# Router logits inside the layer norms, half of the router's one-hot factors as signs on ScalarE, and more buffers for the routed tiles

## The chip, the core and the metric

The kernel runs on one core of one Trainium2 chip. The metric is the device time of one execution in microseconds (us). Three runs of the kernel before gave a median of 1519.82 us (1518.86 to 1523.01). The engines are TensorE (PE in the profile, with PEld for its weight loads), VectorE (DVE), ScalarE (ACT), GpSimd (POOL) and SyncE (SP, which here only issues DMAs and waits). Each engine runs its own program in order, and they meet at semaphores.

## The reference, cut to what matters

Two transformer-like layers over 2048 tokens of width 256. Each is attention over a context, attention or a recurrence over the tokens, and a mixture of experts, and each sub-layer reads a layer norm of x and adds to x. The change touches the layer norms in front of the two mixtures and the mixtures themselves:

```python
# first mixture: x = x + _L0_ffn_ref(_layernorm(x), ...), T=2048, H=256, F=1024, E=8, TOP_K=2
logits = x @ Wg
probs = jax.nn.softmax(logits, axis=-1)
vals, idx = jax.lax.top_k(probs, TOP_K)
weights = vals / (jnp.sum(vals, axis=-1, keepdims=True) + EPS)
hpre = jnp.einsum('th,ehf->tef', x, W1) + b1
act = jax.nn.silu(hpre)
y = jnp.einsum('tef,efh->teh', act, W2) + b2
out = jnp.einsum('te,teh->th', cw, y)          # cw: weights at the chosen experts, else 0
shared = jax.nn.silu(x @ Ws1 + bs1) @ Ws2 + bs2
out = out + SHARED_SCALE * shared

# second mixture: x = x + _L1_ffn_ref(_layernorm(x), ...), E=16, I=192, TOPK=4
logits = jnp.einsum('nh,eh->ne', x, gate_w)
scores = jax.nn.sigmoid(logits)
sb = scores + gate_bias                        # two best groups of four, then four best experts
g = jnp.einsum('nh,eih->nei', x, w1)
u = jnp.einsum('nh,eih->nei', x, w3)
hact = jax.nn.silu(g) * u * combine[:, :, None]
y = jnp.einsum('nei,ehi->nh', hact, w2)
shared = jnp.einsum('ni,hi->nh', jax.nn.silu(x @ ws1.T) * (x @ ws3.T), ws2)
return y + shared
```

## The kernel before

The tokens lie in 16 tiles of 128 (`NT`), kept in SBUF as `k.x` through the whole kernel. A value that has to be exact beyond fp16 is split in two fp16 parts, high and low: ScalarE writes the high part with an ACTIVATE Copy, VectorE the low part as the difference.

The kernel is a chain of blocks, and all engines meet at the end of a block. The blocks that matter here, each once for each mixture:

- **`boundary`** is the layer norm. It goes in 8 steps of two tiles. In a step VectorE takes statistics (L302, L307), the reciprocal (L312) and the normalised rows `xn` (L317); ScalarE writes the high part of the rows (`high`, L258), VectorE the low part (`low`, L321); TensorE transposes both (L221), and ScalarE copies them from PSUM to `n` (`turned`, L266). The rows are also stored to `n_rows` in DRAM, from which the experts gather them later. Two `Boundary` arguments matter: `project`, a function that TensorE calls from its step 3 on, once all tiles of a group of four are in `n`, and `fetch`, which issues the first part of the expert weights.
- **`route`** turns the logits into a placement. TensorE computes the logits (L1025, 16 tiles of 6 small matmuls). Meanwhile ScalarE and VectorE split the first weight slots (`mix.early` of them: `cast_high` L950, `cast_low` L956). Then ScalarE makes the scores (the second mixture's sigmoid, L2134), VectorE chooses the experts (`choose`, from L1693 or L2139) and computes for each choice of each token a slot number, whose upper part (`hi`) says which tile and whose lower part (`lo`) says which row. To invert that map, VectorE writes two one-hot factors for each of the NT x K pairs (32 and 64): `hot_lo` (L1120, 128 wide, times the token's number) and `hot_hi` (L1121, 39 or 79 wide), and TensorE multiplies them into one accumulator (L1035). From it VectorE computes, in a tail (from L1125), the lists `token` and `dest` that the gathers and the scatters use.
- **`first_tiles`** and **`second_tiles`** run the experts. The second has 16 tiles of the shared expert, straight from `n`, and then 79 routed tiles. For these GpSimd gathers 128 rows of `n_rows` for each tile (L1540), TensorE turns them (L1409) and multiplies (L1421), ScalarE takes the SiLU (L1468), VectorE the product with the other half (L1500), the fp16 split of the hidden rows follows (for shared tiles the high part on ScalarE, L1473, for routed ones on VectorE, L1505; the low part L1510, L1511), TensorE turns and multiplies again (L1429, L1436 to L1440), VectorE writes `y` (L1521), and GpSimd scatters it to `y_rows` (L1544). GpSimd has `R` = 32 row buffers; it issues 28 gathers ahead of the first scatter and then mixes the other 51 with the scatters. `y` has 4 buffers, and VectorE waits at L1521 for the scatter that frees one (`t_stored`). The remaining 12 weight slots of the second mixture (17 in all, 1280 wide) are split during the first 12 shared tiles, one in each. At the block's end GpSimd waits for every `t_stored` semaphore.
- **`combine`** then reads `y_rows` back (SP's issues at L1588) and adds them to x with the weights.

In `second_tiles` the order of GpSimd's work comes from these lines:

```python
while gathered < min(R - 4 + (mix.tiles - R + 4) * (s + 1) // (mix.tiles - 12), mix.tiles):
    gather(gathered)
    gathered += 1
scatter(s)
```

## Time and profile before

| | us |
|---|---|
| median of three runs | 1519.82 (1518.86 to 1523.01) |
| profiled execution | 1519.53 |
| its span | 1517.7 |

The blocks around the two mixtures, in the profiled execution, from the span's start:

| block | from | to | us |
|---|---|---|---|
| boundary before the first mixture | 517.0 | 543.2 | 26.2 |
| route of the first mixture | 543.2 | 578.3 | 35.1 |
| tiles of the first mixture | 578.3 | 886.0 | 307.7 |
| boundary before the second mixture | 1138.8 | 1164.9 | 26.1 |
| route of the second mixture | 1164.9 | 1235.6 | 70.7 |
| tiles of the second mixture | 1235.6 | 1467.1 | 231.5 |
| block end and combine | 1467.1 | 1517.7 | 50.6 |

A row of a timeline has the start, the busy time, the engine, the line and operation, what it writes and reads, and in brackets the idle time ahead of it and what ended it. A row with xN stands for N instructions in a run, and its time is that of the whole run. Durations of neighbours overlap a little, so what one more instruction costs is the distance between starts, not the duration. PEclk is the granted clock of TensorE as a share of 2.4 GHz.

### The profile page before, as it was taken

Reading aid. Unit: us, or ns where it says so; the run is one execution under the profiler, and the core shown is the slowest. Engines: PE = TensorE matmul, PEld = TensorE weight load, DVE = VectorE, ACT = ScalarE, POOL = GpSimd, SP = SyncE. Lnnn points to the kernel's source line nnn. Section 1 sums busy time; section 2 is a strip of 40 time slices with the busy share of each in tenths; the row PEclk is TensorE's granted clock in tenths of the full one; section 3 lists DMA queues with packets and bytes.
Section 4 is the critical chain, followed back from the end, with each engine's and each line's share of the span. In section 5 each row is a group of like instructions: output and inputs, shape, how many; then the busy total and the mean of one; then the engine's idle time right before and its main releaser. Section 6 shows DMA issues by size and latency. Waiting matters only on the chain. (4 is left out here: it accounts for less than half of the span.)

```text
span 1517.7 us, 41010 instructions
## 1 busy us (share of the span) xinstructions
PE 1192.2 (79%) x13450; PEld 869.1 (57%) x13450; DVE 1023.9 (67%) x2922; ACT 823.7 (54%) x2124; POOL 450.0 (30%) x480
## 2 busy tenths in 40 slices
PE   5899999998699528999999965966892165999950
PEld 2688888886345417988888842522572033766630
DVE  5699999997656777975544537333657976666636
ACT  6688888885588535854444413411646025666520
POOL 0555555552300000013333210200020037677740
PEclk9999999999899758999999965977995569999975
DMA  3433333332000274001111148298005312233328
GB/s 95 99 78 81 77 81 81 79 79 72 1 1 0 80 294 194 2 16 51 51 51 49 42 149 261 66 350 269 25 1 213 139 35 63 79 105 102 103 71 274
DMA packets 111807, 150.27 MB, mean 99 GB/s; under 512 B 13625, under 2 KB 96962, under 8 KB 111682
## 3 DMA queue, kind: packets, MB, share of 16 engines
q1 hardware_dynamic: 95730, 112.80, 23.8%
q0 software_dynamic: 11328, 30.95, 6.7%
q10 hardware_dynamic: 4624, 4.85, 1.0%
q8 instruction: 78, 1.28, 0.4%
q14 instruction: 47, 0.39, 0.1%
HBM read 126.80 MB, written 21.76 MB: 98 GB/s over the span
## 5 line engine op out<-in xcount | busy, mean ns | idle before, releaser
L1266 ACT ACTIVATE mixture_and_attentions_h<-ps,mixture_and_attentions_b 128x128 f32<-128x128 f32 x440 | 125.6, 373 | 126.2 <-PE ps L1218 124.9
L1218 PE MATMUL ps<-xture_and_attentions_m_w 128*128 128x128 f16 x1872 | 155.7, 219 | 1.8 <-DVE xture_and_attentions_m_w L1296 1.8
L1218 PEld LDWEIGHTS ps<-xture_and_attentions_m_w 128*128 x1872 | 129.1, 98 | 36.2 <-issue 2.6
L1540 POOL DMA_INDIRECT tage_second_mixture_rows<-n_rows,e_second_mixture_r_token x79 | 90.2, 1141 | 140.5 <-SPq L1371 116.7
L641 POOL TENSOR_TENSOR ads_and_recurrence_ctx_s<-ads_and_recurrence_ctx_c,ads_and_recurrence_ctx_s 128x512 f16<-128x512 f32 x64 | 74.2, 1160 | 177.6 <-ACT ads_and_recurrence_ctx_s L570 177.6
L1304 DVE TENSOR_SCALAR ixture_and_attentions_hs<-mixture_and_attentions_h 128x512 f16<-128x512 f32 x110 | 47.2, 429 | 112.7 <-PE ps L1237 97.6
L590 ACT ACTIVATE ads_and_recurrence_probs<-ps,s_and_recurrence_neg_max 128x257 f32<-128x257 f32 x256 | 117.7, 480 | 1.1 <-DVE s_and_recurrence_neg_max L672 1.1
L1236 PE MATMUL ps<-xture_and_attentions_m_w,ixture_and_attentions_hs 128*128 x312 | 117.5, 379 | 0.2 <-DVE xture_and_attentions_m_w L1315 0.2
L1335 POOL DMA_INDIRECT ture_and_attentions_rows<-n_rows,e_and_attentions_r_token x39 | 38.8, 994 | 261.2 <-SPq L1173 162.7
L1421 PE MATMUL ps<-stage_second_mixture_m_w,stage_second_mixture_x_s 128*128 x474 | 92.3, 332 | 2.1 <-issue 1.9
L1544 POOL DMA_INDIRECT y_rows<-stage_second_mixture_y,ge_second_mixture_r_dest x79 | 77.6, 982 | 39.4 <-issue 21.6
L681 DVE TENSOR_SCALAR _heads_and_recurrence_pn<-ads_and_recurrence_probs,heads_and_recurrence_inv 128x256 f32<-128x256 f32 x256 | 79.9, 371 | 8.3
L1237 PE MATMUL ps<-xture_and_attentions_m_w,ixture_and_attentions_hs 128*128 x312 | 85.0, 273 | 0.0
L672 DVE TENSOR_REDUCE s_and_recurrence_neg_max<-ps 128x2 f32<-128x514 f32 x128 | 81.9, 679 | 2.1 <-PE ps L512 2.1
L487 PE MATMUL ps<-ads_and_recurrence_ctx_s,currence_wh_L_xattn_wk_t 128*128 128x256 f16 x512 | 78.3, 276 | 5.1 <-issue 5.1
L1306 DVE SCALAR_TENSOR_TENSOR ixture_and_attentions_hs<-mixture_and_attentions_h,ixture_and_attentions_hs 128x512 f16<-128x512 f32 x110 | 76.2, 693 | 3.8
L520 PE MATMUL ps<-consts_sb,_heads_and_recurrence_pn 128*128 128x128 f32 x512 | 77.0, 273 | 2.2 <-DVE heads_and_recurrence_p_t L688 2.2
L496 PE MATMUL ps<-currence_wh_L_xattn_wv_t,ads_and_recurrence_ctx_s 128*128 128x256 f16 x512 | 77.7, 275 | 0.0
L1339 POOL DMA_INDIRECT y_rows<-xture_and_attentions_m_w,re_and_attentions_r_dest x39 | 38.5, 988 | 131.5 <-DVE xture_and_attentions_m_w L1315 131.2
L635 POOL TENSOR_SCALAR ds_and_recurrence_mask_b<-ds_and_recurrence_mask_i 128x257 bf16<-128x257 int32 x64 | 70.2, 1097 | 5.4
L665 DVE TENSOR_SCALAR ads_and_recurrence_ctx_c<-ads_and_recurrence_ctx_t 128x256 f32<-128x256 f32 x128 | 62.6, 528 | 7.0 <-DMA ads_and_recurrence_ctx_t<-in_ctx_t 7.0
L582 ACT ACTIVATE e_heads_and_recurrence_v<-ps 128x512 f32<-128x512 f32 x64 | 38.2, 597 | 52.5 <-PE ps L531 50.8
(395 smaller groups left out, 3325.4 us busy)
## 6 DMA issues: line engine op xcount, KB each, us to landing
ads_and_recurrence_ctx_t<-in_ctx_t SPq DMA_DIRECT2D x64, 257.0 KB, 2.7
e_and_attentions_b_ctx_t<-in_ctx_t SPq DMA_DIRECT2D x14, 1028.0 KB, 9.2
ure_and_attentions_b_ctx<-in_ctx SPq DMA_DIRECT2D x28, 512.0 KB, 7.8
xture_and_attentions_m_w<-in_m_w SPq DMA_DIRECT2D x2, 5632.0 KB, 37.3
ds_and_recurrence_mask_i<-in_mask SPq DMA_DIRECT2D x256, 32.1 KB, 1.7
stage_second_mixture_c_y<-y_rows SPq DMA_DIRECT2D x16, 512.0 KB, 4.9
stage_second_mixture_m_w<-in_m_w SPq DMA_DIRECT2D x2, 3840.0 KB, 20.5
xture_and_attentions_m_w<-in_m_w SPq DMA_DIRECT2D x1, 5120.0 KB, 16.6
```

The costliest lines, as they stand in the source:

```text
L487: last = pe.matmul(ps[:, KB, m * KR:(m + 1) * KR], w[:, c, m * P:(m + 1) * P], x[:, c, :], start=(n_ == 0), stop=(n_ == len(products) - 1))
L496: last = pe.matmul(ps[:, VB, r * D:(r + 1) * D], x[:, c, r * P:(r + 1) * P], w[:, c, :], start=(n_ == 0), stop=(n_ == len(products) - 1))
L590: act.activation(probs[p][:, j, :], ps[:, SB + j, 0:SK], ACT.Exp, bias=neg_max[:, p, j:j + 1], accum_out=sums[:, p, j:j + 1]).then_inc(k.a ...
L672: dve.tensor_reduce(neg_max[:, p, 2 * h:2 * h + 2], ps[:, SB + 2 * h:SB + 2 * h + 2, 0:SK], AX.X, ALU.max, negate=True).then_inc(k.a_max.s ...
L681: last = dve.tensor_scalar(pn[p][:, j, :], probs[p][:, j, 0:KR], inv[:, p, j:j + 1], None, ALU.mult)
L1218: last = pe.matmul(ps[:, UB + 2 * (u % 2) + f // PER, (f % PER) * P:(f % PER + 1) * P], slots.of(e, c, at, P), a[:, c, :], start=(n == 0), ...
L1236: pe.matmul(ps[:, YB + u % 2, 0:2 * D], h, slots.of(e, block, at, 2 * D), start=(f == 0), stop=False)
L1237: last = pe.matmul(ps[:, YB + u % 2, 0:D], l, slots.of(e, block, at, D), start=False, stop=(f == FC - 1))
L1266: last = act.activation(h32[n][:, at:at + P], ps[:, UB + 2 * (u % 2) + n, at:at + P], ACT.Silu, scale=1 / (WS * NS), bias=b1[:, bass.ds(e ...
L1421: last = pe.matmul(ps[:, UB + u % 2, 0:UP], a[:, c, :], weight(u, w, c * UP, UP), start=(n == 0), stop=(n == len(products) - 1))
L1540: pool.indirect_dma_start(rows[s % R][:, :], None, k.n_rows, bass.IndirectOffsetOnAxis(ap=r.token[:, s:s + 1], axis=0)).then_inc(k.t_rows[ ...
L1544: pool.indirect_dma_start(k.y_rows, bass.IndirectOffsetOnAxis(ap=r.dest[:, s:s + 1], axis=0), y[s % 4][:, :], None).then_inc(k.t_stored[s ...
```

## The change

Five things change.

1. **Logits.** The 96 logits matmuls of each mixture move from `route` into `boundary`, as its `project`: 24 for each group of four tiles, in TensorE's steps 3, 5, 7 and 9.
2. **First weight slots.** Their splits move from `route` into `boundary`: ScalarE's half at the end of its steps 4, 5, ..., VectorE's at the end of steps 5, 6, .... The first mixture keeps 4 such slots; the second has 3 where it had 5, and its other 14 are now split in the first 12 shared tiles.
3. **Router signs.** The factor `hot_hi` of VectorE becomes `side` of ScalarE: the sign of (column − hi − 0.5), one column wider (40 and 80). The difference of two neighbouring columns, halved, is the former one-hot product. It is taken after the accumulation, by one ACTIVATE (`halves`) and one subtraction (`held`). Each factor has 8 buffers where it had 4.
4. **Buffers of `second_tiles`.** 48 row buffers for 32, so 44 gathers are issued ahead of the first scatter for 28, and the other 35 are mixed with the first 59 scatters; 12 `y` buffers and `t_stored` semaphores for 4, so GpSimd waits for 12 at the end of the block. The high part of the hidden rows moves for the 16 shared tiles from ScalarE to VectorE.
5. **Semaphores.** `x_loaded` and `l_rows` become one set, `a_ctx` and `b_ctx_t` another. The waits stand where they stood.

```diff
+                if b.slots and 4 <= s < 4 + b.slots.mix.early:
+                    b.slots.cast_high(act, s - 4)
...
+                if b.slots and 5 <= s < 5 + b.slots.mix.early:
+                    b.slots.cast_low(dve, s - 5)
...
-MIX1 = Mixture(1, E1, K1, 1, 2 * C * I1 + 2 * D, P, 5, (3, 5, 11, 17), 1.0)
+MIX1 = Mixture(1, E1, K1, 1, 2 * C * I1 + 2 * D, P, 3, (3, 5, 11, 17), 1.0)
...
+def logits(k, mix, wg):
+    def project(pe, g, part):
+        if part == 0:
+            for t in range(4 * g, 4 * g + 4):
+                products = [(w, x, c) for w, x in three(wg, (k.n_h, k.n_l)) for c in range(C)]
+                for n, (w, x, c) in enumerate(products):
+                    last = pe.matmul(k.ps[:, 7, t * mix.E:(t + 1) * mix.E], x[:, c, t * P:(t + 1) * P], w[:, c, :], start=(n == 0), stop=(n == len(products) - 1))
+            if g == G - 1:
+                last.then_inc(k.m_logits.sem, 1)
+    return project
...
         def _(pe):
-            for t in range(NT):
-                products = [(w, x, c) for w, x in three(wg, (k.n_h, k.n_l)) for c in range(C)]
...
                     pe.wait_ge(k.m_onehot.sem, k.m_onehot.at(u + 1))
-                    pe.matmul(ps[:, SB, kk * NTL:(kk + 1) * NTL], hot_lo[u % 4][:, :], hot_hi[u % 4][:, :], start=(t == 0), stop=(t == NT - 1)).then_inc(k.m_placed.sem, 1)
+                    pe.wait_ge(k.m_side.sem, k.m_side.at(u + 1))
+                    pe.matmul(ps[:, SB, kk * NTS:(kk + 1) * NTS], hot_lo[u % AHEAD][:, :], side[u % AHEAD][:, :], start=(t == 0), stop=(t == NT - 1)).then_inc(k.m_placed.sem, 1)
...
-            for i in range(mix.early):
-                slots.cast_high(act, i)
             scores(act)
+            act.activation(warm[:, :], k.ident_h[:, 0:1], ACT.Sign)
+            act.wait_ge(k.m_ranked.sem, k.m_ranked.at(1))
+            for kk in range(K):
+                for t in range(NT):
+                    u = kk * NT + t
+                    act.wait_ge(k.m_placed.sem, k.m_placed.at(u - AHEAD + 1))
+                    act.activation(side[u % AHEAD][:, :], iota_h[:, 0:NTS], ACT.Sign, bias=hi_f[:, kk, t:t + 1]).then_inc(k.m_side.sem, 1)
+            act.wait_ge(k.m_placed.sem, k.m_placed.at(NT * K))
+            act.activation(halves[:, :, :].rearrange("p k n -> p (k n)"), ps[:, SB, 0:K * NTS], ACT.Copy, scale=0.5).then_inc(k.m_halved.sem, 1)
...
-            for i in range(mix.early):
-                slots.cast_low(dve, i)
             choose(dve)
...
-                    dve.wait_ge(k.m_placed.sem, k.m_placed.at(u - 3))
-                    dve.tensor_scalar(hot_lo[u % 4][:, :], iota_h[:, :], lo_f[:, kk, t:t + 1], c_["token"][:, t:t + 1], ALU.is_equal, ALU.mult)
-                    dve.tensor_scalar(hot_hi[u % 4][:, :], iota_h[:, 0:NTL], hi_f[:, kk, t:t + 1], None, ALU.is_equal).then_inc(k.m_onehot.sem, 1)
...
+                    dve.wait_ge(k.m_placed.sem, k.m_placed.at(u - AHEAD + 1))
+                    dve.tensor_scalar(hot_lo[u % AHEAD][:, :], iota_h[:, :], lo_f[:, kk, t:t + 1], c_["token"][:, t:t + 1], ALU.is_equal, ALU.mult).then_inc(k.m_onehot.sem, 1)
+
+            dve.wait_ge(k.m_halved.sem, k.m_halved.at(1))
+            dve.tensor_tensor(held[:, :, :], halves[:, :, 1:NTS], halves[:, :, 0:NTL], ALU.subtract).then_inc(k.m_chain.sem, 1)
...
-    R = 32
+    BATCH = 6
+    R, Y = 8 * BATCH, 12
...
-            return range(mix.early + u, mix.early + u + 1) if mix.early + u < mix.count else ()
+            rest, tiles = mix.count - mix.early, NT - 4
+            return range(mix.early + rest * u // tiles, mix.early + rest * (u + 1) // tiles) if u < tiles else ()
...
-                while gathered < min(R - 4 + (mix.tiles - R + 4) * (s + 1) // (mix.tiles - 12), mix.tiles):
+                while gathered < min(R - 4 + (mix.tiles - R + 4) * (s + 1) // (mix.tiles - 20), mix.tiles):
                     gather(gathered)
                     gathered += 1
                 scatter(s)
-            for b in range(4):
-                pool.wait_ge(k.t_stored[b].sem, k.t_stored[b].at((mix.tiles + 3 - b) // 4))
+            for b in range(Y):
+                pool.wait_ge(k.t_stored[b].sem, k.t_stored[b].at((mix.tiles + Y - 1 - b) // Y))
```

ScalarE's program at the end of the second mixture's boundary and through its route, before. `m_w` is the weight slots, `ln_row` the high rows, `sc` the scores:

```order
L258 ACTIVATE stage_second_mixture_ln_row<-stage_second_mixture_ln_xn 128x256 x2
L266 ACTIVATE n<-ps 128x4x128 x2
L172 UNCONDITIONAL_BRANCH
L1037 UNCONDITIONAL_BRANCH
L950 ACTIVATE stage_second_mixture_m_w<-stage_second_mixture_m_w 128x10x128 x5
L2134 ACT_TABLE_LOAD
L2134 ACTIVATE stage_second_mixture_sc<-ps 128x256
L992 UNCONDITIONAL_BRANCH
```

The same place after the change; L260, L264, L268 and L958 are L258, L262, L266 and L950 of before:

```order
L260 ACTIVATE stage_second_mixture_ln_row<-stage_second_mixture_ln_xn 128x256 x2
L264 ACTIVATE stage_second_mixture_ln_sd<-stage_second_mixture_ln_mean,eps 128x2
L268 ACTIVATE n<-ps 128x4x128 x2
L958 ACTIVATE stage_second_mixture_m_w<-stage_second_mixture_m_w 128x10x128
...
L174 UNCONDITIONAL_BRANCH
L1059 UNCONDITIONAL_BRANCH
L2155 ACT_TABLE_LOAD
L2155 ACTIVATE stage_second_mixture_sc<-ps 128x256
L1062 ACTIVATE stage_second_mixture_warm<-ident_h 128x1
L1068 ACTIVATE stage_second_mixture_side<-stage_second_mixture_iota_h,stage_second_mixture_hi_f 128x80 x64
L1070 ACTIVATE stage_second_mixture_halves<-ps 128x320
```

The five slot splits ahead of the sigmoid are gone; three stand inside the boundary (the last of them is shown), and 64 signs and `halves` come behind the sigmoid.

VectorE in the last steps of the same boundary and at the start of the route, before:

```order
L321 TENSOR_TENSOR stage_second_mixture_ln_row<-stage_second_mixture_ln_xn,stage_second_mixture_ln_row 128x256 x2
L172 UNCONDITIONAL_BRANCH
L1047 UNCONDITIONAL_BRANCH
L1049 MEMSET stage_second_mixture_ones_e 128x16
L1050 MEMSET stage_second_mixture_exp_f 128x84
L1051 MEMSET stage_second_mixture_later 128x16x15
L1052 MEMSET stage_second_mixture_later 128x16
L1053 CAST stage_second_mixture_iota_h<-consts_sb 128x128
L956 SCALAR_TENSOR_TENSOR stage_second_mixture_m_w<-stage_second_mixture_m_w 128x10x128 x5
L2139 TENSOR_TENSOR stage_second_mixture_sbias<-stage_second_mixture_sc,nd_mixture_w_L_ffn_gate_bias 128x256
```

After (L325 and L964 are L321 and L956 of before):

```order
L325 TENSOR_TENSOR stage_second_mixture_ln_row<-stage_second_mixture_ln_xn,stage_second_mixture_ln_row 128x256 x2
L964 SCALAR_TENSOR_TENSOR stage_second_mixture_m_w<-stage_second_mixture_m_w 128x10x128
L316 RECIPROCAL stage_second_mixture_ln_sd<-stage_second_mixture_ln_sd 128x2
L321 TENSOR_SCALAR stage_second_mixture_ln_xn<-x_sb,stage_second_mixture_ln_mean,stage_second_mixture_ln_sd 128x256 x2
L325 TENSOR_TENSOR stage_second_mixture_ln_row<-stage_second_mixture_ln_xn,stage_second_mixture_ln_row 128x256 x2
...
L1078 MEMSET stage_second_mixture_ones_e 128x16
L1079 MEMSET stage_second_mixture_exp_f 128x84
L1080 MEMSET stage_second_mixture_later 128x16x15
L1081 MEMSET stage_second_mixture_later 128x16
L1082 CAST stage_second_mixture_iota_h<-consts_sb 128x128
L2160 TENSOR_TENSOR stage_second_mixture_sbias<-stage_second_mixture_sc,nd_mixture_w_L_ffn_gate_bias 128x256
```

The five low halves that stood ahead of the first operation of `choose` (`sbias`) are gone, and the third of the three that are left stands ahead of the last step of the norm.

GpSimd at the start of `second_tiles`, before:

```order
L1540 DMA stage_second_mixture_rows<-n_rows,stage_second_mixture_r_token 128x512 x28
L1544 DMA y_rows<-stage_second_mixture_y,stage_second_mixture_r_dest 18304x256
L1540 DMA stage_second_mixture_rows<-n_rows,stage_second_mixture_r_token 128x512
L1544 DMA y_rows<-stage_second_mixture_y,stage_second_mixture_r_dest 18304x256
L1540 DMA stage_second_mixture_rows<-n_rows,stage_second_mixture_r_token 128x512
L1544 DMA y_rows<-stage_second_mixture_y,stage_second_mixture_r_dest 18304x256
L1540 DMA stage_second_mixture_rows<-n_rows,stage_second_mixture_r_token 128x512
```

After:

```order
L1561 DMA stage_second_mixture_rows<-n_rows,stage_second_mixture_r_token 128x512 x44
L1565 DMA y_rows<-stage_second_mixture_y,stage_second_mixture_r_dest 18304x256
L1561 DMA stage_second_mixture_rows<-n_rows,stage_second_mixture_r_token 128x512
L1565 DMA y_rows<-stage_second_mixture_y,stage_second_mixture_r_dest 18304x256 x2
L1561 DMA stage_second_mixture_rows<-n_rows,stage_second_mixture_r_token 128x512
L1565 DMA y_rows<-stage_second_mixture_y,stage_second_mixture_r_dest 18304x256 x2
```

Sixteen gathers more stand ahead of the first scatter, and behind it two scatters often stand between two gathers.

## Rows read from the trace of the kernel before

**Rows 1.** Windows: busy us of PE, PEld, DVE, ACT, POOL; granted clock, DMA share, GB/s

```profile
1164.90:1235.60 70.70, 19.18 (x163) 9.46 (x164) 64.08 (x269) 7.80 (x8) 0.00 (x0) 0.50 0.33 130
1289.00:1467.10 178.10, 165.44 (x1431) 116.82 (x1429) 114.55 (x398) 103.52 (x237) 127.92 (x130) 0.99 0.31 97
```

**Rows 2.** Timeline, VectorE, first mixture's norm and route's start

```profile
529.73 0.76 DVE L321 TENSOR_TENSOR re_and_attentions_ln_row<-ure_and_attentions_ln_xn,re_and_attentions_ln_row 128x256 f16<-128x256 f32 x2 [0.27 <-ACT re_and_attentions_ln_row L258]
...
543.22 0.07 DVE L1049 MEMSET re_and_attentions_ones_e<- 128x8 f32 x1 [2.54 <-PEq L172]
...
548.94 0.28 DVE L1693 TENSOR_SCALAR ixture_and_attentions_lg<-ps 128x128 f32<-128x128 f32 x1
```

**Rows 3.** Timeline, ScalarE, a step of the same norm

```profile
538.50 1.09 ACT L266 ACTIVATE n<-ps 128x512 f16<-128x512 f16 x2 [0.67 <-PE ps L221]
539.47 0.72 ACT L258 ACTIVATE re_and_attentions_ln_row<-ure_and_attentions_ln_xn 128x256 f16<-128x256 f32 x2
```

**Rows 4.** Groups by line, TensorE, first route: one of its two rows

```profile
L1025 PE MATMUL ps<-d_attentions_wh_L_ffn_Wg,n 128*128 128x8 f16 x64 | 2.6, 168 | 1.7 <-PEq L172 1.7
```

**Rows 5.** Timeline, ScalarE, start of the second route

```profile
1174.53 1.28 ACT L2134 ACT_TABLE_LOAD   x1
1175.83 0.38 ACT L2134 ACTIVATE stage_second_mixture_sc<-ps 128x256 f32<-128x256 f32 x1
```

**Rows 6.** Timeline, VectorE, first operation of the second mixture's choice

```profile
1176.24 0.43 DVE L2139 TENSOR_TENSOR age_second_mixture_sbias<-stage_second_mixture_sc,ixture_w_L_ffn_gate_bias 128x256 f32<-128x256 f32 x1
```

**Rows 7.** Timeline, VectorE, start of the first placement

```profile
564.70 0.31 DVE L1120 TENSOR_SCALAR re_and_attentions_hot_lo<-re_and_attentions_iota_h,ture_and_attentions_lo_f,consts_sb 128x128 f16<-128x128 f16 x1
564.93 0.23 DVE L1121 TENSOR_SCALAR re_and_attentions_hot_hi<-re_and_attentions_iota_h,ture_and_attentions_hi_f 128x39 f16<-128x39 f16 x1
565.07 0.31 DVE L1120 TENSOR_SCALAR re_and_attentions_hot_lo<-re_and_attentions_iota_h,ture_and_attentions_lo_f,consts_sb 128x128 f16<-128x128 f16 x1
```

**Rows 8.** Line L1120, second placement: durations in ns (min/median/max), first and last start

```profile
L1120 DVE TENSOR_SCALAR ge_second_mixture_hot_lo<-ge_second_mixture_iota_h,tage_second_mixture_lo_f,consts_sb x64: 298/302/314, 1208.5 to 1232.1; 128x128 f16<-128x128 f16 x64
```

**Rows 9.** Timeline, ScalarE, four ACTIVATEs with a bias operand

```profile
602.04 1.14 ACT L1266 ACTIVATE mixture_and_attentions_h<-ps,mixture_and_attentions_b 128x128 f32<-128x128 f32 x4 [1.23 <-PE ps L1218]
```

**Rows 10.** Line L950, ScalarE's half of a slot's split, columns as in rows 8

```profile
L950 ACT ACTIVATE xture_and_attentions_m_w<-xture_and_attentions_m_w x36: 1040/1072/1108, 543.2 to 659.8; 128x1024 f16<-128x1024 f32 x36
L950 ACT ACTIVATE stage_second_mixture_m_w<-stage_second_mixture_m_w x17: 1252/1261/1270, 1165.0 to 1284.3; 128x1280 f16<-128x1280 f32 x17
```

**Rows 11.** Timeline, GpSimd, second mixture's tiles

```profile
1247.27 0.94 POOL L1540 DMA_INDIRECT tage_second_mixture_rows<-n_rows,e_second_mixture_r_token  x1 [0.30 <-issue]
1248.52 2.17 POOL L1540 DMA_INDIRECT tage_second_mixture_rows<-n_rows,e_second_mixture_r_token  x1 [0.30 <-issue]
...
1297.79 1.00 POOL L1544 DMA_INDIRECT y_rows<-stage_second_mixture_y,ge_second_mixture_r_dest  x1 [13.56 <-DVE stage_second_mixture_y L1521]
...
1456.38 0.97 POOL L1544 DMA_INDIRECT y_rows<-stage_second_mixture_y,ge_second_mixture_r_dest  x1 [0.30 <-issue]
...
1466.13 0.97 POOL L1544 DMA_INDIRECT y_rows<-stage_second_mixture_y,ge_second_mixture_r_dest  x1 [0.30 <-issue]
```

**Rows 12.** Timeline, VectorE, a slot's low half beside these gathers

```profile
1248.38 1.49 DVE L956 SCALAR_TENSOR_TENSOR stage_second_mixture_m_w<-stage_second_mixture_m_w 128x1280 f16<-128x1280 f32 x1 [0.78 <-ACT stage_second_mixture_m_w L950]
```

**Rows 13.** Chain of waits, second mixture's tiles: us in total, times, longest

```profile
DVE stage_second_mixture_y L1521 <- DMA y_rows<-stage_second_mixture_y,ge_second_mixture_r_dest: 21.5, 22, 2.6
```

**Rows 14.** Timeline, TensorE, where two routed tiles begin

```profile
1290.48 0.39 PE L1409 MATMUL ps<-ident_h,tage_second_mixture_rows 128*128 128x128 f16 x4
...
1292.39 0.39 PE L1409 MATMUL ps<-ident_h,tage_second_mixture_rows 128*128 128x128 f16 x4
```

**Rows 15.** Timeline, GpSimd, last scatter of the first mixture

```profile
885.35 0.97 POOL L1339 DMA_INDIRECT y_rows<-xture_and_attentions_m_w,re_and_attentions_r_dest  x1 [2.18 <-DVE xture_and_attentions_m_w L1315]
```

**Rows 16.** Timeline, SP, first read-back of each mixture

```profile
894.60 2.04 SPq L1588 DMA_DIRECT2D xture_and_attentions_c_y<-y_rows  x4
...
1477.55 2.02 SPq L1588 DMA_DIRECT2D stage_second_mixture_c_y<-y_rows  x4
```

116 lines of the change are left out of this document (57 added, 59 removed).

## The prediction

> **What bounds the kernel now.** I read the windows first, one for each block, since the engines meet at each block's end. Two blocks are touched twice (norm, route) and one once (second tiles). In the second route VectorE is busy 64.08 of 70.70 us, TensorE 19.18 and ScalarE 7.80 [rows 1]: VectorE is the chain, at a granted TensorE clock of 0.50, the lower of its two levels (1.2 GHz). In the routed tiles TensorE is busy 165.44 of 178.10 and GpSimd 127.92 with 130 DMAs [rows 1]. These shares mislead: a GpSimd DMA needs 0.98 us busy and 0.30 before the next, so 123 of them lie between 1297.79 and 1456.38, 1.289 apart [rows 11]. And VectorE waits 22 times, 21.5 us in all, for a scatter to free a `y` buffer [rows 13], while two routed tiles begin 1.91 us apart where nothing holds TensorE [rows 14]. 79 tiles at 1.91 are 151 us; GpSimd's 130 DMAs are 168. So GpSimd bounds this block, though TensorE shows more busy time.
>
> In the norm the timelines show a ring: VectorE's low half, TensorE's transposes, ScalarE's copy, ScalarE's high half, VectorE's low half again. ScalarE waits 0.67 for TensorE and VectorE 0.27 for ScalarE in a step of 2.55 us [rows 2, 3]. Whatever ScalarE puts between its copy and its next high half is on the ring.
>
> **Norms, dearer.** ScalarE's half of a slot takes 1.07 (1024 wide) or 1.26 (1280 wide) [rows 10]; four neighbours of 0.37 take 1.14 [rows 9], so 0.12 of each overlaps, and the steps are 0.95 and 1.14. All stand right behind the copy, on the ring. First mixture: 4 x 0.95 = +3.8. VectorE's halves are about as long and come in the same steps, so they lie beside ScalarE's; the fourth stands behind the last step. Second mixture: ScalarE 3 x 1.14 = 3.4. VectorE's third stands alone ahead of the last step: 1.49 [rows 12] less its overlap of 0.08 (0.31 busy, 0.23 apart [rows 7]) less the 0.27 that it idles: +1.1. Together +4.5. Bounds: nothing, if the ring has more slack than the two idle times say; and +8 and +8 if both halves add up.
>
> **Logits.** 96 matmuls take 2.6 us [rows 4]; the last 24 are 0.65, behind the last copy. The block's end is otherwise held by the store of the last rows, which lands about then, so I take +0.4 for each mixture (0 to 0.7). The other 72 fill TensorE's idle time in the ring.
>
> **Start of the routes, cheaper.** In the first, VectorE starts at 543.22 and comes to its choice at 548.94 [rows 2]. What stands between is memsets, about 0.4, and slot splits. The latter go: -5.3. In the second, ScalarE loads its table at 1174.53, makes the scores at 1175.83, and VectorE follows at 1176.24 [rows 5, 6]. That is 1.7 us, and it now begins with the block at 1164.9 [rows 1]: 1166.6 for 1176.2, -9.6. The fifth and fourth slot waited there for a transfer too; now they are split in the tiles.
>
> **Placement, cheaper.** A pair of factors takes VectorE 0.37 (564.70 to 565.07), of which `hot_lo` is 0.23 (564.70 to 564.93) [rows 7]. First mixture: 32 x 0.14 = -4.5, if ScalarE's 40-wide sign is no slower than 0.23. Second: 63 steps from 1208.5 to 1232.1 are 0.375 each [rows 8]. ScalarE's nearest row, 128 wide with a bias operand, gives (1.14 - 0.37) / 3 = 0.256 [rows 9]. 80 columns need a little less; I take 0.24: 64 x 0.135 = -8.6 (0.23 gives -9.3, 0.256 -7.6). ScalarE then bounds it, by a hair. The tail gets an ACTIVATE out of PSUM and a subtraction, with a handover between: a 512-wide copy is 0.55 to 0.6 [rows 3], so for 80 and 320 columns I add 0.6 and 0.9. The sign's table loads while VectorE chooses, hidden.
>
> What one more ScalarE instruction costs is also on a page. The Trainium skill ("ScalarE: Activation LUTs", "What ACT_TABLE_LOAD costs") gives 280 ns + 0.833 ns a column with a pointer bias, and 93 ns of overlap between neighbours: 0.254 us at 80 columns, by which the second placement would give -7.7 and the sum would be 0.9 higher. The row's 0.256 at 128 columns is below its figure for that width (0.294), so the row decides.
>
> **Tiles of the second mixture, cheaper.** All is on GpSimd. Free gathers start 1.25 apart (1247.27, 1248.52); the one that starts inside VectorE's slot split at 1248.38 takes 2.17 for 0.94, +1.22 [rows 11, 12]. Before: 28 gathers from about 1236.2 to 1284.2, then 13.56 idle until the first `y` [rows 11]. After: 44 x 1.25 + 14 slots x 1.22 = 72.1, so the first scatter is at 1308.3 for 1297.8, +10.5, and nothing idles. Behind it stand 79 scatters and 35 gathers: 114 x 1.289 = 147.0 for the 169.3 from 1297.79 to 1467.10 [rows 11]. -22.3 + 10.5 = -11.8.
>
> Does GpSimd stay fed? When it scatters first, some (1308.3 - 1297.1) / 1.91 = 6 `y` wait. In the mixed part a scatter comes every 94 x 1.289 / 59 = 2.05 us against 1.91 [rows 14], so the lead grows to about 10 of 12 buffers. In the last 20, scatters only, it shrinks by 6 or 7, to 3 or 4 tiles. GpSimd is still the bound, with some 7 us to spare. The shared tiles have two slots more to split in 12 tiles, and the moved high half spares a handover to ScalarE; they must be done by 1308 instead of 1297, which covers both.
>
> Here the page on SBUF speaks against the change. The row: a gather beside the slot split ends with it [rows 11, 12]. The Trainium skill ("SBUF — State Buffer", "SBUF: two separate sides") calls the port pair that VectorE and GpSimd share an exclusive lock, taken for a whole instruction in VectorE's two-port modes, so that the loser waits it out. By that rule the 16 high halves moved to VectorE may hold gathers as well; that is the third rival.
>
> **End of the block.** GpSimd waits for 12 semaphores instead of 4. In the first mixture, with 2, SP goes on 894.60 - 886.32 = 8.3 us after the last scatter; in the second, with 4, 1477.55 - 1467.10 = 10.45 [rows 11, 15, 16]. If the waits made that difference, one costs 1.08 and eight 8.7. Against it: each scatter has a wait of its own in the 0.30 between two DMAs [rows 11]. I take +1.0 (0 to 8.7).
>
> **Semaphores** merged: no instruction changes, 0.
>
> **Sum.** First mixture +3.8 + 0.4 - 5.3 - 4.5 + 0.6 = -5.0. Second +4.5 + 0.4 - 9.6 - 8.6 + 0.9 - 11.8 + 1.0 = -23.2. Together -28.2, from the profiled execution's 1519.5: 1491.3. That execution lies 0.3 below the median, so the same number serves for it.
>
> **Rivals.**
> - *The waits at the end cost 1.08 each.* For it stands the difference of the two ends, against it the 0.30 between DMAs. +7.7 on the forecast: 1499. Chance 0.18.
> - *The tiles give nothing*, because TensorE, turned by gathers that come later or slowed by VectorE's denser work, becomes the bound and ends with GpSimd's old end. The margin of 7 us speaks against it. +11.8: 1503. Chance 0.08.
> - *The moved high halves hold gathers.* 16 at about 0.3 (a 128-wide VectorE operation is 0.31 [rows 7]) are +4.8: 1496. Such halves run on VectorE beside the routed gathers already, and these hold their 1.289. Chance 0.10.
> - *The norms cost both halves in full*, +4 in each, for VectorE's step has little idle time (0.27 [rows 2]): 1499. Chance 0.08.
> - *The norms hide the slot splits.* -8: 1483. Nothing but unseen slack speaks for it. Chance 0.05.
> - *Slower, by the gathers alone.* If the denser VectorE program held each gather, 30 more at 1.22 would put GpSimd +37 behind: 1528. It decides from 23 more blocked ones on (28.2 / 1.22). Before, only those beside a slot split are long, so: chance 0.03.
> - The forecast: 0.48.
>
> The range reaches from the hidden splits to the tiles that give nothing, 1483 to 1503. A measurement tells a change from none beyond about 0.3%, 4.6 us. Only the slower rival and mixtures of several of the dear ones come there: faster 0.95, same 0.02, slower 0.03.
>
> **What the trace after must show.** Norms of about 30.4 and 31.0 us for 26.2 and 26.1, with steps of 3.5 where slots are split. Choices that start 0.4 and 1.7 us into their routes, and factors 0.23 and 0.24 apart. GpSimd without idle time from its first gather to its last scatter, the first scatter some 72 us into the tiles, 158 DMAs in 219 us. Long gathers 14 times. About 11.5 us from the last scatter to SP's read-back. The forecast is wrong if GpSimd waits for `y` anywhere but at the very end, if the norm's steps are over 3.7 us, or if the end of the tiles takes 15 us or more.

## The result, and the profile after

The changed kernel takes 1477.49 us (median of 4 runs, 1475.86 to 1479.54) beside 1520.92 for the kernel before on the same chip: 0.9715 of it, 95% interval 0.9695 to 0.9735. The forecast was 1491.3, range 1483 to 1503: right in sign, too high by 14 us, and outside the range.

The windows of the changed kernel, block by block, with the columns of [rows 1] (norm, route, norm, route, then the second mixture's tiles up to the first scatter, from there to the last, and the rest):

```profile
518.50:548.70 30.20, 10.89 (x160) 9.22 (x160) 23.25 (x78) 20.74 (x47) 0.00 (x0) 0.54 0.44 143
548.70:574.60 25.90, 6.87 (x35) 3.52 (x36) 21.60 (x134) 9.02 (x37) 0.00 (x0) 0.50 0.97 382
...
1134.30:1165.40 31.10, 10.91 (x160) 9.21 (x160) 22.93 (x77) 20.64 (x46) 0.00 (x0) 0.52 0.41 133
1165.40:1219.90 54.50, 15.01 (x66) 6.78 (x66) 48.48 (x201) 18.41 (x68) 0.00 (x0) 0.50 0.43 169
1219.90:1278.90 59.00, 45.69 (x333) 30.02 (x334) 48.39 (x122) 37.98 (x67) 45.02 (x44) 0.91 0.36 97
1278.90:1425.40 146.50, 140.08 (x1315) 107.02 (x1313) 104.18 (x368) 94.98 (x218) 111.94 (x114) 0.99 0.33 104
```

The same two windows of the second mixture's tiles before:

```profile
1235.60:1297.80 62.20, 39.90 (x295) 26.62 (x295) 39.16 (x93) 36.54 (x74) 39.80 (x29) 0.94 0.21 60
1297.80:1467.10 169.30, 156.64 (x1354) 110.16 (x1351) 109.03 (x378) 98.00 (x225) 127.92 (x130) 0.99 0.33 102
```

Part by part this gives, each part counted on VectorE from its first instruction to the first of the next part, the last two on GpSimd and SP (us; the forecast is the sum's terms of the prediction):

| part | before | after | change | forecast |
|---|---|---|---|---|
| first norm | 25.9 | 30.2 | +4.3 | +4.2 |
| first route up to the first factor | 21.5 | 16.1 | -5.4 | -5.3 |
| its placement and tail | 13.3 | 9.4 | -3.9 | -3.9 |
| second norm | 26.1 | 31.1 | +5.0 | +4.9 |
| second route up to the first factor | 43.5 | 33.9 | -9.6 | -9.6 |
| its placement and tail | 26.7 | 20.2 | -6.5 | -7.7 |
| first gather to last scatter | 230.9 | 204.8 | -26.1 | -11.8 |
| last scatter to the read-back | 10.45 | 10.9 | +0.4 | +1.0 |

Seven of the eight terms hold to 1.2 us or better. The eighth, the tiles, is off by 14.3, which is the whole miss. The norms are less sharp than the rest: nine of the traces in this document have the changed kernel's code in the second norm, and it takes 30.2 to 32.0 us in them. GpSimd's timeline after, where [rows 11] had 0.94 and 2.17 in turn, and its last scatter:

```profile
1236.35 0.95 POOL L1561 DMA_INDIRECT tage_second_mixture_rows<-n_rows,e_second_mixture_r_token  x1 [0.30 <-issue]
1237.61 1.20 POOL L1561 DMA_INDIRECT tage_second_mixture_rows<-n_rows,e_second_mixture_r_token  x1 [0.30 <-issue]
1239.11 0.95 POOL L1561 DMA_INDIRECT tage_second_mixture_rows<-n_rows,e_second_mixture_r_token  x1 [0.30 <-issue]
...
1278.99 1.00 POOL L1565 DMA_INDIRECT y_rows<-stage_second_mixture_y,ge_second_mixture_r_dest  x1 [0.30 <-issue]
...
1424.39 0.97 POOL L1565 DMA_INDIRECT y_rows<-stage_second_mixture_y,ge_second_mixture_r_dest  x1 [0.30 <-issue]
```

VectorE beside them (L964 is the slot's low half, L1526 the moved high half of the hidden rows):

```profile
1236.51 1.48 DVE L964 SCALAR_TENSOR_TENSOR stage_second_mixture_m_w<-stage_second_mixture_m_w 128x1280 f16<-128x1280 f32 x1
1237.91 0.35 DVE L1521 SCALAR_TENSOR_TENSOR stage_second_mixture_h<-ps,stage_second_mixture_h 128x192 f32<-128x192 f32 x1
1238.29 0.26 DVE L1526 CAST stage_second_mixture_hs<-stage_second_mixture_h 128x192 f16<-128x192 f32 x1
...
1239.26 1.48 DVE L964 SCALAR_TENSOR_TENSOR stage_second_mixture_m_w<-stage_second_mixture_m_w 128x1280 f16<-128x1280 f32 x1
```

The gather of 1237.61 starts while the low half of 1236.51 runs. That ends at 1237.99, the gather 0.82 later, at 1238.81. Before, the one of 1248.52 started 0.14 into the low half of 1248.38, which ended at 1249.87, and the gather ended 0.82 later, at 1250.69 [rows 11, 12]. The rule is the same and the price is not: what a gather loses is what is left of the low half when it starts, less 0.13 (it takes 0.95 alone and ends 0.82 behind the low half). And a shared tile, from low half to low half, takes 1239.26 - 1236.51 = 2.75 us, where before it took 3.73 (1252.10 - 1248.38). The tile before, as a chain from VectorE's product over ScalarE's high half and slot split to the next low half:

```profile
1249.78 0.35 DVE L1500 SCALAR_TENSOR_TENSOR stage_second_mixture_h<-ps,stage_second_mixture_h 128x192 f32<-128x192 f32 x1
1250.17 0.36 ACT L1473 ACTIVATE stage_second_mixture_hs<-stage_second_mixture_h 128x192 f16<-128x192 f32 x1 [1.60 <-DVE stage_second_mixture_h L1500]
1250.81 1.26 ACT L950 ACTIVATE stage_second_mixture_m_w<-stage_second_mixture_m_w 128x1280 f16<-128x1280 f32 x1
1252.10 1.49 DVE L956 SCALAR_TENSOR_TENSOR stage_second_mixture_m_w<-stage_second_mixture_m_w 128x1280 f16<-128x1280 f32 x1 [0.78 <-ACT stage_second_mixture_m_w L950]
```

Two gathers in step with a tile are 0.95 + 0.30 + g + 0.30 = the tile: g is 2.18 for 3.73 and 1.20 for 2.75.

The two lines of the placement, with the columns of [rows 8]:

```profile
L1147 DVE TENSOR_SCALAR ge_second_mixture_hot_lo<-ge_second_mixture_iota_h,tage_second_mixture_lo_f,consts_sb x64: 303/308/315, 1199.4 to 1214.0; 128x128 f16<-128x128 f16 x64
L1068 ACT ACTIVATE tage_second_mixture_side<-ge_second_mixture_iota_h,tage_second_mixture_hi_f x64: 343/344/362, 1199.4 to 1215.3; 128x80 f16<-128x80 f16 x64
```

VectorE's last factor starts at 1214.0, ScalarE's at 1215.3: ScalarE bounds it, at 15.9 / 63 = 0.252 us a sign, where I took 0.24.

### The profile page after: what moved, and what is told of

It is laid out like the page before. It is cut to its first block and busy times, and to the rows that moved or that the text cites. A ratio compares the mean times of both kernels' runs of the same rounds, so it can differ in the third digit from the quotient of the medians.

```text
span 1476.2 us, 41116 instructions
## 1 busy us (share of the span) xinstructions
PE 1179.2 (80%) x13450; PEld 870.8 (59%) x13450; DVE 1013.1 (69%) x2844; ACT 843.3 (57%) x2208; POOL 438.5 (30%) x480
## 5 line engine op out<-in xcount | busy, mean ns | idle before, releaser
L1561 POOL DMA_INDIRECT tage_second_mixture_rows<-n_rows,e_second_mixture_r_token x79 | 79.6, 1007 | 129.3 <-SPq L1399 105.6
L641 POOL TENSOR_SCALAR ds_and_recurrence_mask_b<-ds_and_recurrence_mask_i 128x257 bf16<-128x257 int32 x64 | 70.2, 1097 | 5.4
```

Source lines behind the costliest of these rows:

```text
L1561: pool.indirect_dma_start(rows[s % R][:, :], None, k.n_rows, bass.IndirectOffsetOnAxis(ap=r.token[:, s:s + 1], axis=0)).then_inc(k.t_rows[ ...
```

## The experiments

The theories. **A**: GpSimd's gathers run in step with the shared tiles; the moved high half made those shorter, and that is what the sum lacked. **B**: the hold is a fixed price for a slot's split, and another edit made it smaller. The first four runs brought a second question: **C**, that the routed tiles needed a line of the change that the prediction passed over (the form of the weights' address), against **D**, that they did not.

Times stand beside the kernel before on the same chip. The first four runs found it at 1518.83 us. All later ones fell on chips where the kernel before takes 1593 to 1600. In which block the difference lies is told under the fifth to seventh run; what makes it was not found.

**The high half back on ScalarE.**

```diff
+            def high(u):
+                act.wait_ge(k.t_gated.sem, k.t_gated.at(u + 1))
+                act.wait_ge(k.t_flip.sem, k.t_flip.at(u - 2))
+                act.activation(hs[u % 3][:, 0:I1], h32[u % 3][:, :], ACT.Copy).then_inc(k.t_high.sem, 1)
...
+                if u + 3 < NT:
+                    high(u + 3)
```

> The changed kernel with one part undone: the high half of the hidden rows of the 16 shared tiles is on ScalarE again. Theory A (the gathers are paced by the shared tile): a gather that starts while VectorE works on a slot's low half waits for its end, GpSimd then falls into step with the tiles, two gathers to a tile, and the moved high half counts because it shortened the tile from 3.73 us to 2.75. Then the period is 3.7 us or more again, every second gather takes about 2.2 us for 1.20, the first scatter comes 72 us behind the first gather for 58.4, and the time is 13 to 14 us more, about 1491. Theory B (the hold is short because of the other edits: more gathers, another order of the slots' splits, another form of the weights' address): the gathers stay at 0.95 and 1.20 and the time within 3 us of 1477.5.

Measured 1486.05 us, 0.9789 of before (0.977 to 0.9807): less dear than the 1491 that I expected from A, and well clear of B. The gathers are back at 0.95 and 2.17, one pair to a tile of 3.73:

```profile
1234.92 0.95 POOL L1569 DMA_INDIRECT tage_second_mixture_rows<-n_rows,e_second_mixture_r_token  x1 [0.31 <-issue]
1236.17 2.17 POOL L1569 DMA_INDIRECT tage_second_mixture_rows<-n_rows,e_second_mixture_r_token  x1 [0.30 <-issue]
1238.65 0.95 POOL L1569 DMA_INDIRECT tage_second_mixture_rows<-n_rows,e_second_mixture_r_token  x1 [0.30 <-issue]
```

The first scatter comes 70.2 us behind the first gather (58.4 in the changed kernel), the routed part is the same (146.2 and 146.4), and first gather to last scatter is 216.4: 11.6 more. The prediction's sum for this block was 219.1. It describes this kernel, the changed one without the moved high half, to 3 us (70.2 for 72.1 to the first scatter, 146.2 for 147.0 behind it). The times agree with 11.6: 0.9789 less the changed kernel's 0.9715 is 0.0074 of 1519, 11.2 us.

**A longer shared tile.**

```diff
+        extra = k.sb("extra", [P, D], ctx=ctx)
...
                 if u < NT:
+                    dve.tensor_scalar(extra[:, :], out, 1 / (WS * HS), None, ALU.mult)
                     dve.scalar_tensor_tensor(k.x[:, u, :], out, mix.shared_weight / (WS * HS), k.x[:, u, :], ALU.mult, ALU.add)...
```

> The changed kernel with one more VectorE instruction in each of the 16 shared tiles, a 256-wide copy out of PSUM that nothing reads, 0.42 us long and some 0.33 from start to start. It has no operand in SBUF to read. Theory A (gathers in step with the tiles): the tile's period goes from 2.755 to about 3.09, and though nothing that holds GpSimd was added, every second gather grows by the same 0.33, from 1.20 to 1.53; over 12 tiles the first scatter comes 4 us later (62.4 behind the first gather) and so does the end: 1481.5. Theory B (each slot's low half or high half costs a gather a fixed time): gathers stay at 1.20, first scatter at 58.4, and the time stays at 1477.5, since GpSimd bounds the block and the first y has 4.8 us of room.

Measured 1479.61 (0.9734, 0.9717 to 0.975). That interval and the changed kernel's (0.9695 to 0.9735) overlap, so the trace decides. Beside the low halves every second gather, eleven in all, went to 1.53 or 1.54:

```profile
1231.48 1.54 POOL L1563 DMA_INDIRECT tage_second_mixture_rows<-n_rows,e_second_mixture_r_token  x1 [0.30 <-issue]
1233.33 0.94 POOL L1563 DMA_INDIRECT tage_second_mixture_rows<-n_rows,e_second_mixture_r_token  x1 [0.30 <-issue]
1234.57 1.53 POOL L1563 DMA_INDIRECT tage_second_mixture_rows<-n_rows,e_second_mixture_r_token  x1 [0.30 <-issue]
```

First scatter at 62.0 us (forecast by A 62.4, by B 58.4), first gather to last scatter 208.4 for 204.8. The added instruction reads PSUM alone, and it holds nobody: the other gathers start 0.24 before its end and take 0.94 or 0.95. Yet it made the held ones longer by what it adds to the tile, 0.33. B falls, A holds.

**The moved high half alone, on the kernel before.** The edit is the first one turned round.

> The kernel before with one part of the change alone: the high half of the 16 shared tiles on VectorE. Theory A: period 2.75 for 3.73, every second gather 1.20 for 2.17. The 28 gathers end after about 38 us, but the first scatter waits for the first y, which comes 54 us behind the first gather for 60.9; the routed part is as before (169). So 7 us less: about 1514. Theory B: gathers as before at 2.17, the first y somewhat earlier; 0 to 7 us less as well, so here the length of the gathers tells, not the time.

Measured 1505.48 us, 0.9898 (0.9879 to 0.9918). The gathers are 0.95 and 1.20. The first `y` comes 49.4 us behind the first gather for 60.9, the first scatter at 50.1 for 61.6, and the block takes 219.8 for 230.9. I had expected 7 us and the block gives 11: twelve tiles shorter by 0.97 each. By the times it is 13 to 15. This one edit, which the prediction priced at nothing, gives more alone than the buffers alone do (next run).

**The buffers alone, on the kernel before.**

```diff
-    R = 32
+    BATCH = 6
+    R, Y = 8 * BATCH, 12
...
-                while gathered < min(R - 4 + (mix.tiles - R + 4) * (s + 1) // (mix.tiles - 12), mix.tiles):
+                while gathered < min(R - 4 + (mix.tiles - R + 4) * (s + 1) // (mix.tiles - 20), mix.tiles):
```

> The kernel before with the buffers alone: 48 row buffers, 12 y buffers, 44 gathers ahead (and the merged semaphores, which free the eight that this needs). My prediction's term for the tiles was made for this case: a hold of 1.22 for each slot split. Both theories agree on the period of 3.73 and gathers of 2.17 here: 44 x 1.255 + 12 x 1.22 = 69.9 to the first scatter, then 114 x 1.289 = 147, 217 us for 230.9, and 8 more waits at the end at 0 to 1 us: about 13 us less, 1507. If it gives 20 us or more, the buffers themselves did more than GpSimd's sum says; if it gives less than 8, TensorE or the y become the bound without the shorter tile.

Measured 1515.22, 0.9972 (0.9954 to 0.999): about 4 us of the 13. The first scatter is where the sum puts it, at 69.9. But the routed part takes 156.5 and not 147, and GpSimd waits:

```profile
POOL y_rows L1549 <- DVE stage_second_mixture_y L1526: 17.4, 24, 1.5
```

The `y` come 161.8 / 78 = 2.07 us apart, and TensorE waits for other engines only 1.2 us in all in these 156.5. So TensorE bounds the routed tiles here. That is the condition of the prediction's second rival, though the block still gives 4.5 us (226.4 for 230.9). In the changed kernel they come 145.0 / 78 = 1.86 apart, with the same buffers. What differs in TensorE's own program of this block is one helper, `weight`, which forms the address of an expert's weights. In the order of instructions before, a routed tile's products are

```
L1421 ISA
L1421 MATMUL ps<-stage_second_mixture_m_w,stage_second_mixture_x_s 128x384
L1421 REGISTER_ALU
L1421 MATMUL ps<-stage_second_mixture_m_w,stage_second_mixture_x_s 128x384 x3
L1421 ISA
L1421 MATMUL ps<-stage_second_mixture_m_w,stage_second_mixture_x_s 128x384
L1421 ISA
```

and after, with the offset inside the slice,

```
L1450 ISA
L1450 MATMUL ps<-stage_second_mixture_m_w,stage_second_mixture_x_s 128x384
L1450 REGISTER_ALU
L1450 MATMUL ps<-stage_second_mixture_m_w,stage_second_mixture_x_s 128x384 x3
L1450 REGISTER_ALU
L1450 MATMUL ps<-stage_second_mixture_m_w,stage_second_mixture_x_s 128x384
L1450 REGISTER_ALU
```

Two of the steps between matmuls are a plain register addition now.

The first run belongs beside this one. It is on the same chip, and the code of its block differs from this one's in two places: `weight`, and the slots that are split beside the shared tiles (14 for 12, all done 16 us or more ahead of the first scatter in both traces). Its high halves are on ScalarE too. There the routed part takes 146.2 us for 156.5, and the `y` come 1.86 apart. So neither the high halves nor the slots explain the 2.07. What is left is the address, or something that the other blocks' edits change in this one.

**The old address in the changed kernel.**

```diff
-                both = slots.of(expert(u), 0, 2 * lo + x * P, 2 * n).rearrange("p (b x n) -> p b x n", x=2, n=P)
-                return both[:, :, 0, :]
+                both = slots.of(expert(u), 0, 2 * lo, 2 * n).rearrange("p (b x n) -> p b x n", x=2, n=P)
+                return both[:, :, x, :]
```

> The changed kernel with one line undone: TensorE's address of an expert's weights is again formed as before (the low part is picked out of a slice by its index, so an instruction that needs a new register computes it with one more step), instead of by an offset inside the slice. Theory C, from the run with the buffers alone: the y there came 2.07 us apart (78 steps in 161.8 us), in the changed kernel 1.86 (145.0), because TensorE's own program holds its matmuls; this line is the third part without which the buffers give little. Then the y come 2.07 apart here too, the first at 53.6 us and the last at 215.4 behind the first gather, the last scatter at about 218 for 204.8: +13, 1490.5. Rival D: the pace of the run with the buffers alone came from something else there (ScalarE's high halves until late, the slots' splits, the order of the gathers): the y stay 1.86 apart and the time within 2 us of 1477.5.

**Buffers and new address on the kernel before.**

> The kernel before with the buffers and the new address form, nothing else. Theory C: the first scatter stays 69.9 us behind the first gather, the routed part falls from 156.5 to 147, GpSimd's own 114 x 1.289: some 9.5 us less than with the buffers alone, about 1506, 13 us under the kernel before. Rival D: no different from the buffers alone, 1515.

**The new address alone.**

> The kernel before with the new address form alone. GpSimd and its 4 y buffers bound the routed part there, with only about 2 us of waits for y in it. Theory C: 0 to 3 us less, 1516 to 1519, so the line is worth nothing by itself. If TensorE bound the routed part of the kernel before, it would give 0.2 us a tile, up to 16 us less.

These three gave 1573.91 us (0.9839), 1596.86 (0.9988) and 1600.39 (0.9996, 0.9978 to 1.0015), with the kernel before at 1600.27. The norms, routes and block ends took what they take in the first traces to about 1 us, and the first gather starts within 6 us of where it did. The second mixture's tiles did not: first gather to last scatter 306, 306 and 311 us where 205 to 231 stood. The engines stand still there in long pieces behind which the trace shows no releaser. In the old-address run TensorE's longest:

```profile
1270.56 0.40 PE L1465 MATMUL ps<-stage_second_mixture_m_w,stage_second_mixture_h_t 128*128 128x256 f16 x1 [27.42 <-issue]
```

Small differences between kernels in this block can't be read from such a time. The first two kernels were run again three times, once with the changed kernel beside them:

> The changed kernel with the old form of the weights' address, again: on the chip of the first try every kernel, the one before too, stood still for 10 to 50 us at a time in the second mixture's tiles, with engines waiting for nothing that the profile shows. Theory C (TensorE's own instruction stream bounds the routed tiles at 2.07 us with the old form, 1.86 with the new): last scatter about 218 us behind the first gather for 204.8, some 13 us over the changed kernel on the same chip. Rival D (the 2.07 of the run with the buffers alone came from something else there): within 2 us of the changed kernel.

> The kernel before with the buffers and the new address form, again. Theory C: first scatter 69.9 us behind the first gather, routed part 147 for the 156.5 of the buffers alone, 1519 - 14 = 1505 if the chip gives 1519 for the kernel before. Rival D: 156.5, 1515.

> The changed kernel, unaltered, beside the others on one chip: 0.9715 of the kernel before, 204.8 us from the first gather to the last scatter of the second mixture. All theories expect the same; it is the base for the next run and for the old address.

The standstills came each time. Old address: 1576.74 (0.9873), then 1571.5 (0.9867), then 1572.21 (0.9861). Buffers and address: 1597.06 (0.9985), 1589.64 (0.9973), 1590.16 (0.9982). The changed kernel itself: 1576.03 us, 0.9844 (0.9809 to 0.988), with 309.4 us from first gather to last scatter. On that chip the old address cost nothing (1576.74 beside 1576.03, and 305.8 beside 309.4 us for the block), so where the standstills are, it does not set the time. What C and D forecast for a chip without them was never measured with one line alone. What the traces do give is the distance between the starts of two routed tiles on TensorE, 78 in each run, of which the standstills touch only a part:

```
                                        median   under 1.95 us
kernel before                             2.03              8
its high half on VectorE                  2.06              6
buffers alone                             2.03              4
changed kernel                            1.91             75
changed, high half on ScalarE             1.91             75
with standstills:
changed kernel                            1.98             38
changed, the last three edits  1.91, 1.92, 1.91         43, 40, 43
changed, old address           2.14, 2.08, 2.02, 2.11   16, 12, 20, 13
before, buffers, new address   1.92, 1.94, 1.91, 1.91   42, 40, 48, 44
before, new address alone                 2.12             38
```

The kernel before, and with its high half on VectorE, is bound by GpSimd and its `y` buffers too, so their distances are not all TensorE's own. With the new form a tile that nothing holds takes 1.91 us, and where there are no standstills nearly all do; with the old one few come to it. The counts sort by the address, on both kinds of chip. With the pair of runs above this speaks strongly for C. That the 10 us between their routed parts come from the address is an inference from that pair; no undisturbed run changes the address alone.

The third and fourth tries had been expected so:

> The changed kernel with the old form of the weights' address. In the two tries so far only 12 and 16 of 78 distances between routed tiles were under 1.95 us, against 75 in the undisturbed trace of the changed kernel. Theory C: on an undisturbed chip TensorE then runs at 2.07 a tile and GpSimd waits for it: last scatter 215 to 218 us behind the first gather for 204.8, 1488 to 1491. Rival D: 205 and 1478.

> The kernel before with the buffers and the new address form. Theory C: first scatter at 69.9 us, routed part 147 for 156.5, 1505. Rival D: 156.5 and 1515.

> The changed kernel with the old form of the weights' address. Theory C, on a chip without the long standstills: last scatter 215 to 218 us behind the first gather for 204.8, 1488 to 1491. Rival D: 205 and 1478.

> The kernel before with the buffers and the new address form. Theory C: first scatter at 69.9 us, routed part 147 for 156.5, 1505. Rival D: 156.5 and 1515.

**One early slot for three.** `MIX1`'s `early` is 1.

> The changed kernel with one early slot in the second mixture for three; the other 16 are split in the first 12 shared tiles. The norm gets ScalarE's 1.14 and VectorE's 1.1 instead of 4.6 us: -2.3. The tiles: two more splits on VectorE, 1.4 each, but GpSimd bounds them; by theory A a gather waits only for what is left of a split, and a longer tile takes it in: +0.5 to +2.8 until the first scatter. In all -2 to +0.5 us.

Measured 1570.84 us, 0.9818 (0.9789 to 0.9847), with no changed kernel on that chip to set beside it. The second norm took 29.9 us where nine traces with three slots give 30.2 to 32.0: a gain of 0.4 to 2.1 for the expected 2.3. The tiles had their standstills.

**One early slot, and in the last steps.**

```diff
-                if b.slots and 4 <= s < 4 + b.slots.mix.early:
-                    b.slots.cast_high(act, s - 4)
+                if b.slots and H - b.slots.mix.early <= s < H:
+                    b.slots.cast_high(act, s - H + b.slots.mix.early)
...
-                if b.slots and 5 <= s < 5 + b.slots.mix.early:
-                    b.slots.cast_low(dve, s - 5)
+                if b.slots and H - b.slots.mix.early < s:
+                    b.slots.cast_low(dve, s - 1 - H + b.slots.mix.early)
```

> The changed kernel with one early slot in the second mixture for three, and the early splits of both norms in the last steps instead of from the fourth on: ScalarE's last in step 7, VectorE's last behind its last low rows, where it idles 2.8 us until the block ends. For the first mixture (4 slots) nothing moves. Second norm: only ScalarE's 1.14 is left on the ring for 4.6 us in all, so 27.7 us for 31.1. Second tiles: 16 splits in 12 tiles for 14; by theory A the gathers stay in step and the first scatter comes 0.5 to 2.8 us later. In all -3 to -0.5 us against the changed kernel. If the norm hardly gets shorter, something other than the ring sets it.

Measured 1571.46 beside the changed kernel's 1576.03, 0.9835 (0.9807 to 0.9863) for 0.9844: no difference that these times can tell. The norm is 29.3 us beside 32.0 of the changed kernel on that chip. That is 2.7 less of the 3.4 forecast, but the 27.7 that I had named did not come, and against the shortest of the nine traces it is 0.9. VectorE's half now lies where it waited for the block's end anyway:

```profile
1154.75 0.76 DVE L325 TENSOR_TENSOR ge_second_mixture_ln_row<-age_second_mixture_ln_xn,ge_second_mixture_ln_row 128x256 f16<-128x256 f32 x2 [2.12 <-ACT ge_second_mixture_ln_row L260]
1155.43 1.48 DVE L964 SCALAR_TENSOR_TENSOR stage_second_mixture_m_w<-stage_second_mixture_m_w 128x1280 f16<-128x1280 f32 x1
1158.32 0.07 DVE L1078 MEMSET ge_second_mixture_ones_e<- 128x16 f32 x1 [1.41 <-PEq L174]
```

**No low halves beside the tiles.**

```diff
+        if self.mix.n == 1 and i >= self.mix.early:
+            dve.memset(self.split(i, 1), 0.0).then_inc(k.t_wlow.sem, 1)
+            return
```

> The changed kernel, but the low halves of the 14 slots that are split beside the tiles are not computed: VectorE fills them with zeros instead, so the experts' weights are only their high parts. The fill reads nothing from SBUF. Theory A: what a gather waits for is an instruction of VectorE with two operands in SBUF that runs when it starts; with none as long as that left, gathers take 0.95 to 1.0 us but where they start in one of the short ones, and 44 of them take 55 to 56 us for 58.4. If a gather is held by any long VectorE instruction, or by the high halves, every second one is still 1.1 or more.

One execution: 1558.62 us beside 1593.77 for the kernel before, again with standstills. None of the 44 gathers was over 1.00 us; in the changed kernel with standstills two were, 1.57 and 1.47, each beside a low half. Only two of the fills fell among the gathers here, so this agrees with A and is no strong test of it. The two held gathers of the changed kernel's trace follow the rule: they started at 1233.65 and 1249.32, in low halves that ended at 1234.39 and 1249.96, and ended at 1235.22 and 1250.79, 0.83 behind each.

One row speaks against what I had expected, that only an instruction with two operands in SBUF holds a gather. The one gather of 1.00 us starts inside a moved high half, which reads a single one:

```profile
1267.33 1.00 POOL L1564 DMA_INDIRECT tage_second_mixture_rows<-n_rows,e_second_mixture_r_token  x1 [0.30 <-issue]
1267.25 0.26 DVE L1529 CAST stage_second_mixture_hs<-stage_second_mixture_h 128x192 f16<-128x192 f32 x1
```

It ends at 1268.33, again 0.82 behind the end of the CAST (1267.51). A gather that started at 1251.04 inside a fill with 0.46 left took 0.95.

## Why the prediction was wrong

**The norms, the routes, the block's end: right.** The ring was read rightly: ScalarE's half of a slot cost 0.95 a step, VectorE's lay beside it. VectorE's steps with both are 3.5 us as forecast (534.76 to 538.28 in the first norm). The eight waits more at the end cost 0.4 us, so the first rival (1.08 each) is out. The third (16 holds of about 0.3) is out as well, since the gathers got shorter, not longer. Its mechanism exists, as the last run's CAST shows, but at 0.05 us for that gather; in the changed kernel none of the first 44 gathers starts inside a moved high half. The norms hid nothing and cost no second half.

**The second placement: mechanism right, size off.** I took 0.24 for a sign; it is 0.252, and the tail +1.1. The figures of the Trainium skill ("ScalarE: Activation LUTs", "What ACT_TABLE_LOAD costs") gave an estimate of 0.254 for 80 columns, and the trace agrees (0.252). I set it aside for a row at 128 columns out of PSUM, which it did not fit; the operands here lie in SBUF.

**The tiles: the step that failed.** It is "44 x 1.25 + 14 slots x 1.22 = 72.1", and with it the sentence that the moved high half "spares a handover to ScalarE", which "covers" the two slots more. I read the gather as ending with the low half, and took its 1.22 for a price of the low half; it ends 0.82 behind it. The 1.22 is what was left of it when the gather started (less 0.13), and in steady state it is the shared tile's period less two free gathers: 3.73 - 2.51 = 1.22. A shorter tile makes it smaller: 2.75 - 2.51 = 0.24. The moved high half cuts the tile by 0.97, because in the kernel before VectorE's product, ScalarE's high half, its slot split and VectorE's low half stand in one chain; after, VectorE's own work fills the tile. Measured: with the high half on ScalarE 216.4 us for the block, with it on VectorE 204.8. The high half alone on the kernel before gives 11.1 us. Of the 14.3 us that the term lacked, 11.6 are the moved high half (216.4 - 204.8); the other 2.7 lie in the sum without it, 219.1 for the 216.4 measured.

**TensorE's pace: an error that another one hid.** The prediction read 1.91 us a tile from one pair of starts [rows 14] and made the margin of 7 us from it. That pair was among the best of the old form: the median of the 78 distances of the kernel before is 2.03, and with the buffers alone TensorE, at 2.07, took 9.5 us of the gain back. TensorE was the bound there, as the second rival has it, though it did not take the whole gain. In the changed kernel the pace is 1.91 in 75 of 78, as the prediction has it, most likely by the edit of `weight`, to which it gave no line. The first run and the one with the buffers alone leave little else (146.2 and 156.5 us), but no undisturbed run has that line alone, so it is argued and not shown. That the prediction's pace came true in the changed kernel is luck: it was read from rows of the kernel before, which seldom keeps it.

The changed kernel's block by parts, first gather to last scatter: before 230.9, buffers alone 226.4, high half alone 219.8, all but the high half 216.4, all 204.8.

Open: what the standstills on the later chips are, and what they would do with other code. There every kernel that was traced takes 300 to 311 us for this block (290 without the low halves), the changed one 309.4 and the one before with the new address 311.0. In the changed kernel 43.5 us of the difference lie ahead of the first scatter, where TensorE stands 10.2, 23.9 and 10.8 us while GpSimd issues its gathers, and 61.1 behind it. So the tiles' edits are worth little there, and the change keeps mainly what it gains elsewhere, 15.7 us in the table above; the times are 1600.44 and 1576.03. The kernel before itself has no trace on those chips.

## What to carry to other kernels

When two engines stand in step, a wait that repeats is a remainder, the one's period less the other's own work; price it as that, and ask of every edit what it does to the period, on engines off the chain too. An edit on the engine that is not the bound is not free of effect when the bound engine waits in step with it. And take an engine's free pace from the spread of all its tiles, not from one pair, above all where the engine's own stream computes addresses between its instructions.

## What the runs showed of the hardware that was not expected

- A gather on GpSimd that starts while VectorE runs a slot's low half, an instruction with two SBUF operands, ends 0.82 us after that instruction, whether 1.35 us, 0.74, 0.64 or 0.38 of it were left. A CAST from SBUF to SBUF with 0.18 left did the same (1.00 us for 0.95). Instructions that read PSUM held nothing with up to 0.34 left, and a MEMSET nothing with 0.46 left. The Trainium skill ("SBUF — State Buffer", "SBUF: two separate sides") has the lock that these rows show: it names VectorE's two-port modes and instructions with two SBUF inputs.
- The kernel before took 1519 us on the chip of the first four runs and 1593 to 1600 on four others; the changed kernel took 1477 and 1576. In the changed kernel's traces all of the difference lies in one block (309.4 us for 204.8). In that block TensorE stood for up to 24 us at a time, VectorE and ScalarE for up to 18, and TensorE for 27 with the old address, while GpSimd's gathers kept their 1.25 us. The cause stays open.
